# Edge records assembled ahead of a GpSimd scatter, and loaded as whole rows by it

## The reference, cut to what matters

```python
row, col = edge_index[0], edge_index[1]                 # src, dst
d_raw = (edge_weight / CUTOFF)[:, None]                 # CUTOFF = 5.0
edge_input = jnp.concatenate([x[row], x[col], edge_attr, d_raw], axis=-1)   # edge_attr: 16 wide
h = jax.nn.silu(edge_input @ ew1 + eb1)
m_ij = jax.nn.silu(h @ ew2 + eb2)
agg = jax.ops.segment_sum(m_ij, row, num_segments=x.shape[0])
```

## Time and profile before

| | us |
|---|---|
| median of 3 runs | 6490.53 |
| lowest and highest of them | 6486.48, 6493.28 |
| profiled execution, its own time | 6465.67 |
| span of its profile | 6464.0 |
| busy: PE, PEld | 4506.1, 3917.8 |
| busy: DVE, ACT, POOL | 3365.5, 1498.8, 3893.9 |

### The profile page before, as it was taken

How to read it: one execution, slowest core, us unless ns; L and a number is a source line. 1 busy time by engine, 2 the same in 40 slices (tenths; PEclk the granted TensorE clock), 3 DMA queues, 4 the chain that set the end, 5 groups by cost and what they waited for, 6 DMA issues and landing times. The chain is left out here.

```text
span 6464.0 us, 125959 instructions
## 1 busy us (share of the span) xinstructions
PE 4506.1 (70%) x41113; PEld 3917.8 (61%) x41114; DVE 3365.5 (52%) x5567; ACT 1498.8 (23%) x2045; POOL 3893.9 (60%) x3580
## 2 busy tenths in 40 slices
PE   0000477766555535868694699999999999984995
PEld 0000266652222215858583599999999999973995
DVE  6898744457777741121310355555555555543333
ACT  0000000016666672000000122222222222221441
POOL 0000288888888887777877277777777777740000
PEclk9999699998888877969897699999999999986996
DMA  0400355543333348949794344444444444443882
GB/s 15 169 0 10 65 104 102 103 70 106 95 92 92 92 113 271 349 121 356 244 343 148 83 117 117 118 117 118 118 117 117 117 118 118 118 70 47 232 231 69
DMA packets 907314, 840.46 MB, mean 130 GB/s; under 512 B 326597, under 2 KB 816113, under 8 KB 903660
## 3 DMA queue, kind: packets, MB, share of 16 engines
q1 hardware_dynamic: 788028, 684.65, 34.6%
q0 software_dynamic: 119216, 154.89, 12.6%
HBM read 680.88 MB, written 156.42 MB: 130 GB/s over the span
## 5 line engine op out<-in xcount | busy, mean ns | idle before, releaser
L996 POOL DMA_INDIRECT out_records<-nodes_scatter_recs,nodes_scatter_rows x1650 | 1947.9, 1181 | 493.6 <-issue 493.6
L1738 POOL DMA_INDIRECT edge_mlp_b_rows<-b_table,edge_mlp_recs x1664 | 1583.7, 952 | 637.3 <-issue 414.5
L1241 PE MATMUL build_p_ring<-build_hot_near,build_hot_far 128*128 128x392 f16 x2400 | 553.2, 383 | 407.3 <-issue 224.5
L1241 PEld LDWEIGHTS build_p_ring<-build_hot_near,build_hot_far 128*128 128x128 bf16 x2400 | 255.0, 106 | 705.2 <-issue 608.5
L1792 PE MATMUL edge_mlp_p_pre<-edge_mlp_hot_t,edge_mlp_a_blk 128*128 128x128 f32 x3328 | 670.6, 283 | 8.5 <-DMA edge_mlp_b_rows<-b_table,edge_mlp_recs 6.6
L1793 PE MATMUL edge_mlp_p_pre<-c_ident,edge_mlp_b_rows 128*128 128x128 f32 x3328 | 646.1, 276 | 0.0
L1326 PE MATMUL sum_x_p_main<-sum_x_parts,sum_x_tiles 128*128 128x192 bf16 x5488 | 477.0, 251 | 226.5 <-DVE sum_x_parts L1269 178.9
L1852 DVE CAST edge_mlp_hot_t<-edge_mlp_p_turned 128x512 f32<-128x512 bf16 x416 | 287.8, 692 | 632.4 <-PE edge_mlp_p_turned L1784 632.4
L1326 PEld LDWEIGHTS sum_x_p_main<-sum_x_parts,sum_x_tiles 128*128 128x128 f16 x5488 | 466.2, 100 | 237.2 <-issue 187.2
L1127 PE MATMUL sums_p_sum<-sums_attr,sums_hot 128*128 x3328 | 450.4, 293 | 191.3 <-issue 172.0
L1761 PE MATMUL edge_mlp_p_m<-edge_mlp_w,edge_mlp_h 128*128 128x128 f32 x3328 | 576.2, 295 | 1.7 <-ACT edge_mlp_h L1819 1.7
(11 more groups left out here) (444 smaller groups left out, 6553.2 us busy)
## 6 DMA issues: line engine op xcount, KB each, us to landing
sum_x_tiles<-edge_counts SPq DMA_DIRECT2D x168, 768.0 KB
edge_mlp_a_blk<-a_table SPq DMA_DIRECT2D x1664, 64.0 KB
edge_counts<-build_plane SPq DMA_DIRECT2D x28, 3136.0 KB, 9.8
sum_z_tiles<-edge_counts SPq DMA_DIRECT2D x49, 1792.0 KB, 8.7
sum_y_tiles<-edge_counts SPq DMA_DIRECT2D x84, 768.0 KB
sums_attr<-in_edge_attr SPq DMA_DIRECT2D x100, 512.0 KB, 4.3
sum_x_tiles<-edge_counts SPq DMA_DIRECT2D x56, 832.0 KB
out_records<-place_padding SPq DMA_DIRECT2D x104, 256.0 KB, 2.1
```

The costliest lines, as they stand in the source:

```text
L996: pool.indirect_dma_start(out=out_rec, out_offset=bass.IndirectOffsetOnAxis(ap=rows[s][:, c:c + 1], axis=0), in_=recs[s][:, c], in_offset= ...
L1241: pe.matmul(p_ring[:, ds(banks[c], 1), 0:KEYS], hot_far[s][:, c // 2, :, c % 2], hot_near[s][:, c // 2, :, c % 2], start=False, stop=True, ...
L1738: pool.indirect_dma_start(out=b_rows[s][:, c], out_offset=None, in_=b_tab, in_offset=bass.IndirectOffsetOnAxis(ap=recs[s][:, c, FE + 1:FE ...
```

## The change

- `tables_in` keeps one DVE operation: the low bits of src, into a new table `a.low`. The three operations that wrote `edge_meta` go, and `edge_meta` with them.
- `place_out` puts the records together in edge order. For 11 pieces of 125 x 150 edges, SP loads the 16 attributes, ACT writes weight / 5, dst, low bits and attributes into one of two buffers of whole records (four operations), and SP stores the buffer to a new HBM array `lin_rec`, in edge order. POOL clears the two buffers first. Then SP pads the rest of `lin_rec` (4,950 records, four DMAs) and fills `out_records` with padding as before, behind the assembly in its queue. The row table `edge_row` covered all 128 partitions already before: for the three without edges it points at spare rows behind the records.
- `scatter_records`: the load of a piece is 25 whole records for each of 128 partitions (3,200 contiguous bytes each) from `lin_rec`. The clearing, the copy of `edge_meta` and the branch on `unsorted` are gone. The 25 indirect DMAs per piece are the same.

```diff
@@ tables_in
-            step(dve.tensor_scalar(a.meta[0:EP, :, 0], a.weight[:], 1.0 / CUTOFF, None, ALU.mult))
-            step(dve.tensor_copy(a.meta[0:EP, :, 1].bitcast(I32), a.ends["in"][:]))
-            step(dve.tensor_scalar(a.ints[:], a.ends["out"][:], P - 1, None, ALU.bitwise_and))
-            step(dve.tensor_copy(a.meta[0:EP, :, 2], a.ints[:]))
+            step(dve.tensor_scalar(a.low[:], a.ends["out"][:], P - 1, None, ALU.bitwise_and))
@@ place_out, sync
+            def assemble(source16):
+                attrs = source16.rearrange("(p c) w -> p c w", p=EP)
+                def load(j):
+                    if j >= 2:
+                        sp.wait_ge(made[j % 2], 4 * (j // 2))
+                    sp.dma_start(attr[j % 2][:], attrs[:, j * WIDE:(j + 1) * WIDE]).then_inc(attr_in[j % 2], 16)
+                load(0)
+                for j in range(pieces):
+                    if j + 1 < pieces:
+                        load(j + 1)
+                    sp.wait_ge(made[j % 2], 4 * (j // 2 + 1))
+                    sp.dma_start(lines[0:EP, j * WIDE:(j + 1) * WIDE], recs[j % 2][:]).then_inc(stored[j % 2], 16)
...
             sp.wait_ge(pad_set, 2)
+            for lo in range(0, (P - EP) * EC // P, PRE):
+                width = min(PRE, (P - EP) * EC // P - lo)
+                sp.dma_start(spare[:, lo:lo + width], padding[:, 0:width]).then_inc(prefilled, 16)
+            rest = (P - EP) * EC % P
+            sp.dma_start(lin_rec[P * EC - rest:P * EC], padding[0:rest, 0]).then_inc(prefilled, 16)
@@ place_out, scalar
+            act.wait_ge(cleared, 2)
+            for j in range(pieces):
+                s, at = j % 2, slice(j * WIDE, (j + 1) * WIDE)
+                if j >= 2:
+                    act.wait_ge(stored[s], 16 * (j // 2))
+                act.mul(recs[s][:, :, FE], a.weight[:, at], 1.0 / CUTOFF).then_inc(made[s], 1)
+                act.copy(recs[s][:, :, FE + 1].bitcast(I32), a.ends["in"][:, at]).then_inc(made[s], 1)
+                act.copy(recs[s][:, :, FE + 2], a.low[:, at]).then_inc(made[s], 1)
+                act.wait_ge(attr_in[s], 16 * (j // 2 + 1))
+                act.copy(recs[s][:, :, 0:FE], attr[s][:]).then_inc(made[s], 1)
@@ place_out, gpsimd
+            for s in range(2):
+                nc.gpsimd.memset(recs[s][:], 0.0).then_inc(cleared, 1)
@@ scatter_records
-        for s in range(3):
-            nc.gpsimd.memset(recs[s][:], 0.0).then_inc(cleared, 1)
-        pool.wait_ge(cleared, 3)
...
-                pool.dma_start(recs[s][0:EP, :, 0:FE], recs_of[:, at]).then_inc(rec_in[s], 16)
-                nc.gpsimd.tensor_copy(recs[s][0:EP, :, FE:FE + 3], meta[0:EP, at]).then_inc(staged[s], 1)
+            pool.dma_start(recs[s][:], lines[:, at]).then_inc(rec_in[s], 16)
```

More of the change, by code:

```diff
@@ L25 @@
 PIECES = EC // SC
+WIDE = 150
 IN_REC = F + 2 + FE + 1
@@ L921, in _, with place_out @@
                 act.copy(k["low"][:, i * P:(i + 1) * P], of[:, P:2 * P]).then_inc(key_out, 1)
-def place_out(nc, k, a, out_rec):
+def place_out(nc, k, a, lin_rec, out_rec, ea16, in_rec):
     with ExitStack() as ctx:
@@ L930, in place_out @@
         padding = sb("padding", [P, PRE, OUT_REC])
+        attr = [sb(f"attr{s}", [EP, WIDE, FE]) for s in range(2)]
+        recs = [sb(f"recs{s}", [EP, WIDE, OUT_REC]) for s in range(2)]
         pad_set, prefilled, chain, spare_set = sem("pad_set"), sem("prefilled"), sem("chain"), sem("spare_set")
+        cleared, attr_in, made, stored = sem("cleared"), *([sem(f"{n}{s}") for s in range(2)] for n in ("attr_in", "made", "stored"))
+        pieces = EC // WIDE
+        lines = lin_rec.rearrange("(p c) w -> p c w", p=P)
         block = st.block()
@@ L963, in _, with scatter_records @@
                                           op0=ALU.mult, op1=ALU.add))
-def scatter_records(nc, k, together, recs, rows, meta, row, ea16, in_rec, out_rec, signals):
-    cleared, rec_in, staged, passed, scattered = signals
+def scatter_records(nc, k, together, recs, rows, row, lin_rec, out_rec, signals):
+    rec_in, staged, passed, scattered = signals
+    lines = lin_rec.rearrange("(p c) w -> p c w", p=P)
     @together.block.gpsimd
     def _(pool):
-        for s in range(3):
-            nc.gpsimd.memset(recs[s][:], 0.0).then_inc(cleared, 1)
-        pool.wait_ge(cleared, 3)
[L980 to L986, removed]
-                pool.dma_start(recs[s][0:EP, :, 0:FE], recs_of[:, at]).then_inc(rec_in[s], 16)
-                nc.gpsimd.tensor_copy(recs[s][0:EP, :, FE:FE + 3], meta[0:EP, at]).then_inc(staged[s], 1)
[L989 to L1009, removed]
@@ new lines, in stage, with send @@
+        def stage(i, s, done):
+            at = ds(i * (3 * SC) + s * SC, SC)
+            wait_count(pool, scattered[s], done * (16 * SC))
+            turnstile(pool, k["gate"], s, passed)
+            pool.dma_start(recs[s][:], lines[:, at]).then_inc(rec_in[s], 16)
+            nc.gpsimd.tensor_copy(rows[s][:], row[:, at]).then_inc(staged[s], 1)
+        def send(i, s):
+            pool.wait_ge(rec_in[s], i * 16 + 16)
+            pool.wait_ge(staged[s], i + 1)
+            turnstile(pool, k["gate"], s, passed)
+            for c in range(SC):
+                pool.indirect_dma_start(
+                    out=out_rec, out_offset=bass.IndirectOffsetOnAxis(ap=rows[s][:, c:c + 1], axis=0),
+                    in_=recs[s][:, c], in_offset=None).then_inc(scattered[s], 16)
@@ L1010, in scatter @@
+        rounds = PIECES // 3
+        stage(0, 0, 0)
+        for i in steps(pool, rounds - 1):
             stage(i, 1, i)
@@ L1013, in scatter @@
             send(i, 1)
+            stage(i + 1, 0, i + 1)
             send(i, 2)
[L1016 to L1021, removed]
+        i = rounds - 1
+        stage(i, 1, i)
+        send(i, 0)
+        stage(i, 2, i)
+        send(i, 1)
+        send(i, 2)
         for s in range(3):
@@ L2035, in right @@
                 return to.enter_context(nc.sbuf_tensor(name, shape, dt, side="right"))
[L2037 to L2038 removed]
+            row = right(both_ctx, "edge_row", [P, EC], I32)
+            passed = ctx.enter_context(nc.semaphore("recs_passed"))
             rec_in, staged, scattered = ([ctx.enter_context(nc.semaphore(f"recs_{n}{s}")) for s in range(3)]
@@ L2050, in gnn_stack @@
             a = EdgeArrays(nc, edges_ctx)
-            a.iota, a.meta, a.row = k["iota"], meta, row
+            a.iota, a.row = k["iota"], row
             check_order(nc, k, a, src, dst, weight)
@@ L2055, in gnn_stack @@
             count_out(nc, k, a)
-            place_out(nc, k, a, out_rec)
+            place_out(nc, k, a, lin_rec, out_rec, ea16, in_rec)
             edges_ctx.close()
```

21 lines of the change are left out of this document (16 added, 5 removed).

## The result

On the chip of the first comparison the changed kernel takes 6273.92 us (median of 4 runs, 6270.63 to 6274.29) against 6491.9 (4 runs): ratio 0.9662, 95% interval 0.9645 to 0.9679, 218 us less. On a second chip the same kernel is 12% slower than the kernel before; that came out in the experiments and is told there.

A forecast was written before the change was run, and what follows sets the result against it. POOL's scatters and loads were taken as the longer of two chains by some 74 us. The meeting 176 us earlier, tables_in -3.8 and clearing +3 make -177: 6490.5 becomes 6313, rounded 6315, range 6285 to 6425.

The forecast's parts named there:

- the meeting: Where POOL's scatters and the work of PE, DVE and ACT join before the next stage: forecast 3372 instead of 3547.9.
- the step from profiles to medians: Whole kernel: 177 us less takes the profiled 6465.67 to 6289; taken off the median 6490.5 it gives 6313, rounded 6315.
- the relief of the other chain: PE with DVE and ACT, from plan to in-passes: cheaper loads end it 102 us earlier, at 3368 (3318 to 3470).
- the passes 50 of 70.4: Three in-passes: of PE's 70.4 us of waits for tiles, 50 come back (0 to 70).
- Sums 48: Sums stage: 3 of the 4.6 us lost behind each of 16 loads come back, 48 us (0 to 74).
- Build 4: Build stage: only short delays of ACT found behind loads, so 4 us come back (0 to 8).
- POOL's chain: POOL's 1,650 scatters and 66 loads: gains 211 us, 18 given back beside build, ending at about 3349 instead of 3542.
- The start: POOL before its first load, 774.6 to 786.25: clearing and branch go, up to 11.7 us less.
- Rival 1: Only the tail goes: the other engines' work stays at 3470.2, 74 us less, 6416; chance 0.15.
- rival 2: The load stays at 3.84 us on POOL, which gains only 24 us: 6466; chance 0.05.
- Cover: Place stage: assembly and padding done at 573, hidden 53 us before DVE, which sets the stage's length.
- Rivals 3 and 4: Place stage: stores at half rate outgrow DVE's time, 6462, chance 0.06; or stores get one engine, 7077, chance 0.04.

The follow-up runs named there:

- the doubled store: Changed kernel, every assembled piece stored a second time into an array that nobody reads: 9518.09 us, ratio 1.1344 against the kernel before.

## Why the forecast was too high

The sign and the mechanism were right: dearer small loads go, both chains shorten, and the meeting of the two comes earlier. Two terms of the sum were mis-sized, and they make up the miss of 41 us: the step from profiles to medians (25 us) and the relief of the other chain, which put the meeting too late (15 us). The rest is the rounding of 6313.5 to 6315.

**The reference point, 25 us of the 41.** The forecast took 177 us, read from the profile, off the median 6490.5, as if both kernels' profiles lay equally far from their medians. But the profiled execution of the kernel before lay 25 us below its median, and that of the kernel after lies on its own (6274.29 for 6273.92). The profiles differ by 191.4, the medians by 218. Why the one profile lay low stays open. Against the profiles alone, 6289 was forecast and 6274 came.

**The other chain.** The step "so the other chain ends 102 us earlier, at 3368" failed. It ended 227 us earlier, at 3243. Its terms: the passes 50 of 70.4, in fact 102 (the three take 240.6, 240.5 and 238.1 us instead of 276, 275.5 and 269.9). All 70.4 us of waits for tiles went, and PE's busy time in the passes fell by 31 us more, which the forecast had put at nothing. Sums 48, in fact 59. Build 4, in fact 68, the worst of them: I looked for waits behind each load in build and found few, but the mean of its matmuls fell from 383 to 363 ns, their "issue" idle time from 224.5 to 165.4 us, while their waits for ACT grew from 170.4 to 199.9, and the clock was higher. A cost spread over every instruction doesn't show as a wait behind the load. I didn't separate how much of it is the clock.

**POOL's chain, right at its end, by terms that cancel.** Forecast end 3349, measured 3339.25. The load was priced at 1.0 us, its upper neighbour; it is 0.58, 28 us better over 66. The start gave some 22 us rather than 11.7, since the forecast looked only as far as the first load, and the second had 11.34 us of idle time before it. Against these 38 us the scatters cost 53 us rather than 18. That term was wrong in kind too: it expected 30 scatters more beside the slow build stage, and there are 30 fewer, each slower. A few microseconds more came off with the copies. So the small error of the end is partly luck. The Trainium skill (DMA: Bandwidth & Descriptors, section on the anatomy of one DMA) has descriptor generation small. With 3.84 us for 3,125 runs, and 1.58 against 0.58 us for the same bytes in 3,200 runs and in 128, the traces don't bear this out.

**The meeting.** I had two nearly level chains and took the other one's 3372; the text names POOL's own meeting as 3355, if the relief is greater. That is what came: 3349.39, 10.1 us after the last scatter rather than 5.95. So 198.5 us came off, not 176, and 7.1 were lost behind it. One sign of the forecast went the other way with it: DVE's idle time before the next stage was to fall below 15 us, and it rose to 106.3, because POOL alone sets the meeting now. PE's waits for tiles were to be near 20 us, and there are none. Rival 1, that the other chain wouldn't move, is out; rival 2 (load dear) too.

**Place and tables.** Cover held, as forecast; assembly and padding ended at about 544 for 573. The clearing beside the first compare cost 3.6 us for 3. The Trainium skill (SBUF — State Buffer, section Who interferes with whom) has DVE in its two-port fast modes and GpSimd exclude each other for a whole instruction. The trace agrees: the first clearing ends 4.1 us after its start, the later compares, with nothing of POOL's beside them, take 1.08, and the first compare takes 4.93 and ends 0.9 us after that clearing, so it lost nearly all of the clearing's time. `tables_in` gave 4.05 for 3.8. Rivals 3 and 4 fall with the doubled store's 134 GB/s.

**What the forecast didn't have at all** is the second kind of chip, on which the sign is the other one. The seed stood in the profile: in the sums stage PE's idle time was put down to "issue", a wait with no owner, and PE stood still for up to 3.35 us ahead of a batch behind a load. Shown is that on that kind an unbroken row of scatters holds PE to about one matmul per two scatters, that less work on POOL makes it worse (1.126), and that one pause of 4.6 us per 25 scatters brings the changed kernel level with the kernel before (0.997), both still 1,700 to 1,900 us above their times on the first kind. What PE, DVE and SP lack in such a row, and why chips differ in it, no run here shows.

## What to carry to other kernels

Price a GpSimd load by how it is cut up, not by its bytes: 0.58 us for 128 runs of 3,200 bytes, 1.58 for the same bytes in 3,200 runs, 3.84 for half of them in 3,125 runs of 64 on 125 partitions. Where an engine's idle time is "issue" beside another engine's dense row of indirect DMAs, treat that as contention with an unknown bound, and measure the change on more than one chip before trusting its sign. And set a forecast against the profiled execution's own time: state both, and give the gap between it and the median as a term of its own.

## What was unexpected of the hardware

- One kernel, two kinds of chip: 6490 and 8376 us for the same code, with the same pace of POOL's scatters (1181 and 1184 ns).
- Removing loads from POOL's chain slowed the kernel before from 8376 to 9417 us; adding 304 us of clearings to the changed kernel's chain took it from 9423 to 8191 (with 8386 and 8219 for the kernel before beside them).
- A clearing of 216 columns in front of a scatter takes 0.29 us, but the scatter's idle time is 0.14 us shorter with it (497.2 to 272.5 us over 1,650) and its busy time 0.07 (2000.9 to 1887.4), so that some two thirds of it are free. The build stage differs between the two kernels as well, so the part in the busy time may not be the clearing's.
